# Grouped-query attention with an FFN on one NeuronCore: the value products of a group's last two pairs move to the next slot

## The reference

```python
# attention: 32 query heads, 8 key/value heads, head size 128
q = rope(layernorm(x) @ Wq);  k = rope(ctx @ Wk);  v = ctx @ Wv
attn = softmax(where(mask == 0, -1e9, q k^T / sqrt(128)))
x = x + concat_heads(attn @ v) @ Wo
# feed-forward: routed scales around a matrix of signs
h = layernorm(x)
routing = softmax(h @ gate_w.T)
out = (h * (routing @ in_scale)) @ sign(weight).T * (routing @ out_scale) + bias
x = x + out
```

## Time and profile before

| | |
|---|---|
| median of three executions | 1199.98 us (1199.96 to 1200.46) |
| the profiled execution | 1200.44 us, its span 1197.4 us |
| PE busy | 1162.7 us, 97% |
| VectorE busy | 810.1 us, 68% |
| GpSimd busy | 712.2 us, 59% |
| ScalarE busy | 551.7 us, 46% |
| mean granted TensorE clock | 0.988 |
| DMA, mean over the span | 89 GB/s |

### The profile page before, as it was taken

How to read it: one execution, slowest core, us unless ns; L and a number is a source line. 1 busy time by engine, 2 the same in 40 slices (tenths; PEclk the granted TensorE clock), 3 DMA queues, 4 the chain that set the end, 5 groups by cost and what they waited for, 6 DMA issues and landing times.

```text
span 1197.4 us, 23749 instructions
## 1 busy us (share of the span) xinstructions
PE 1162.7 (97%) x7636; PEld 951.1 (79%) x7636; DVE 810.1 (68%) x1367; ACT 551.7 (46%) x1768; POOL 712.2 (59%) x593
## 2 busy tenths in 40 slices
PE   5799999999999999999999999999999999999996
PEld 4588888888888888887888888888888888888875
DVE  6767677666776666676766677667667666666663
ACT  3445445444453544444544444544454354444432
POOL 5666655555666655765555675655666565676515
PEclk8899999999999999999999999999999999999997
DMA  8234332232422223433322322323332221222200
GB/s 219 86 110 119 96 98 87 80 92 80 120 89 71 79 79 88 128 101 93 98 76 72 95 90 77 105 80 96 88 98 88 62 79 62 87 83 89 66 2 35
DMA packets 136923, 106.02 MB, mean 89 GB/s; under 512 B 12776, under 2 KB 111080, under 8 KB 136864
## 3 DMA queue, kind: packets, MB, share of 16 engines
q1 hardware_dynamic: 131488, 94.78, 27.0%
q10 hardware_dynamic: 4608, 8.39, 2.1%
q0 software_dynamic: 768, 2.10, 0.5%
HBM read 101.05 MB, written 4.19 MB: 88 GB/s over the span
## 4 chain that ended last, share of the span: by engine, by line
PE 87%; DVE 9%; POOL 2%; issue 1%; ACT 1%; DMA 1%; POOLq 0%; DVEq 0%; SPq 0%; ACTq 0%
PE chunk L1037 23%; PE chunk L1038 22%; PE chunk L1039 22%; PE o_ps L1110 4%; DVE swp L793 3%; PE sc_ps L1085 3%; PE tr_ps L1085 2%; PE aux L1026 2%; PE o_ps L1026 2%; DVE qT L795 1%; PE sc_ps L1026 1%; PE tr_ps L1026 1%; PE aux L1187 1%; PE aux L1188 1%; DVE oT_lo L728 1%
## 5 line engine op out<-in xcount | busy, mean ns | idle before, releaser
L404 POOL TENSOR_TENSOR w_lo<-raw,w_hi 128x512 fp32r<-128x512 f32 x192 | 247.2, 1299 | 385.3 <-ACT w_hi L503 385.3
L793 DVE TENSOR_TENSOR swp<-chunk,sinT 64x512 f32<-64x512 f32 x320 | 220.4, 689 | 98.7 <-PE chunk L1039 94.7
L1037 PE MATMUL chunk<-xT_hi,w_hi 128*128 128x512 f32 (+1 forms) x512 | 211.6, 413 | 2.0 <-POOL w_lo L404 1.9
L1038 PE MATMUL chunk<-xT_lo,w_hi 128*128 128x512 f32 (+1 forms) x512 | 201.9, 394 | 0.0
L1039 PE MATMUL chunk<-xT_hi,w_lo 128*128 128x512 f32 (+1 forms) x512 | 201.1, 393 | 0.0
L1037 PE MATMUL chunk<-wo_hi,oT_hi 128*128 128x512 f32 x496 | 196.6, 396 | 0.4 <-issue 0.4
L411 POOL TENSOR_TENSOR qT<-qT,swp 128x512 f32<-128x512 f32 x128 | 165.9, 1296 | 47.1 <-DVE qT L795 44.9
L1039 PE MATMUL chunk<-wo_hi,oT_lo 128*128 128x512 f32 x496 | 193.7, 390 | 0.0
L1038 PE MATMUL chunk<-wo_lo,oT_hi 128*128 128x512 f32 x496 | 193.2, 390 | 0.0
L539 ACT ACTIVATE probs<-scores,neg_max 128x64 f32<-128x64 f32 x512 | 170.4, 335 | 28.2 <-DVE neg_max L750 28.2
L735 DVE TENSOR_TENSOR acc<-chunk,acc 128x512 f32 (+1 forms) x128 | 88.2, 689 | 139.9 <-PE chunk L1039 139.5
(11 more groups left out here) (281 smaller groups left out, 1936.7 us busy)
## 6 DMA issues: line engine op xcount, KB each, us to landing
raw<-in_L_xattn_Wo SPq DMA_DIRECT2D x132, 256.0 KB, 2.6
raw<-in_L_xattn_Wq SPq DMA_DIRECT2D x128, 256.0 KB, 2.7
raw<-in_L_xattn_Wk SPq DMA_DIRECT2D x32, 256.0 KB
raw<-in_L_xattn_Wv SPq DMA_DIRECT2D x32, 256.0 KB
acc<-in_x ACTq DMA_DIRECT2D x16, 256.0 KB, 2.9
c_tile<-in_ctx SPq DMA_DIRECT2D x12, 256.0 KB, 3.1
x_tile<-in_x SPq DMA_DIRECT2D x12, 256.0 KB, 3.4
result<-y ACTq DMA_DIRECT2D x12, 256.0 KB, 2.1
```

What stands on the lines that cost most here:

```text
L404: nc.gpsimd.tensor_tensor(lo, raw[:, n % RING, :], hi.bitcast(F32), ALU.subtract).then_inc(wsplit_lo, 1)
L793: last = nc.vector.tensor_tensor(swp[to, k, :], bank[of, :], sinT[to, here], ALU.mult)
L1037: nc.tensor.matmul(bank, a_hi, b_hi, start=i == 0, stop=False)
L1038: nc.tensor.matmul(bank, a_hi, b_lo, start=False, stop=False)
```

## The change

The block `values(s, 1)`, the value products of a group's pairs 2 and 3, leaves its place between `project(3)` and `project(4)` and runs in the next slot, between `out_proj(0)` and `v_rows`, through a small class `SlotBefore` that has the number of the slot before. What takes its output moves along: `out_hi` 2 and 3 on ScalarE to the place ahead of `v_in_rows`, `out_lo` 2 and 3 on VectorE to the place ahead of `v_lo_split`. Since the `o_ps` banks are in use then, V's transposes get a bank of their own, `chunk[2]`: `v_rows` waits for the last rotation out of that bank, and `out_proj(2)`, the next to write to it, waits for `v_ok`. `t_rows` and `values(s, 0)` get waits for the subtractions out of the `o_ps` banks. In FFN slots `scale_in` goes from behind `rotate(2)` to ahead of it. GpSimd's and SyncE's queues stay as they are. The diff shows `slot(s)` of ScalarE, VectorE and TensorE in this order; their `attend_last(s)` get the same added lines at the same places, on ScalarE behind its four `split_hi`.

```diff
-        DUO_BANK, V_BANK, TABLE_BANK = [sc_ps, tr_ps], o_ps[0], o_ps[1]
+        DUO_BANK, V_BANK, TABLE_BANK = [sc_ps, tr_ps], chunk[2], o_ps[1]
...
+        class SlotBefore:
+            def __init__(self, s):
+                self.U = s.U - 1
+                self.late = True
...
             def out_hi(s, p):
                 act.wait_ge(pv_done, (s.U - 1) * DUOS + p // 2 + 1)
-                if not s.first_attn:
+                if s.late:
+                    act.wait_ge(outproj_done, (s.U - 1) * PAIRS + 1)
+                elif not s.first_attn:
...
             def slot(s):
...
                     split_hi(s, 1)
+                if s.wo:
+                    out_hi(SlotBefore(s), 2)
+                    out_hi(SlotBefore(s), 3)
                 if s.attn:
                     v_in_rows(s)
...
                     xs_split(f[0], in_slot)
-                if s.attn:
-                    out_hi(s, 2)
-                    out_hi(s, 3)
-                if s.ffn:
                     out_scales(f[0], in_slot)
...
             def slot(s):
...
                     add_out(s, 0)
+                    out_lo(SlotBefore(s), 2)
+                    out_lo(SlotBefore(s), 3)
                 if s.attn:
                     v_lo_split(s)
...
                     out_lo(s, 1)
+                if s.ffn:
+                    scale_in(f[0], in_slot)
                 if s.proj:
                     rotate(s, 2)
-                if s.ffn:
-                    scale_in(f[0], in_slot)
...
                     rotate(s, 3)
-                if s.attn:
-                    out_lo(s, 2)
-                    out_lo(s, 3)
...
                 elif p == 1:
                     pe.wait_ge(vT_ok, s.U)
+                elif p == 2:
+                    pe.wait_ge(v_ok, s.U)
...
             def v_rows(s):
                 pe.wait_ge(vT_ok, s.U)
-                if not s.first_attn:
-                    pe.wait_ge(o_lo, (s.U - 1) * PAIRS)
+                pe.wait_ge(cos_done, s.U * KQ)
...
                 if d == 0:
                     pe.wait_ge(v_ok, s.U)
+                    if not s.first_attn:
+                        pe.wait_ge(o_lo, 2 * n)
...
-            def t_rows(t):
+            def t_rows(s, t):
                 pe.wait_ge(rows_in, 16 * (t - PAIRS + 1))
+                if s.wo:
+                    pe.wait_ge(o_lo, (s.U - 1) * PAIRS)
...
             def slot(s):
...
                     out_proj(s, 0)
+                    values(SlotBefore(s), 1)
                 if s.attn:
                     v_rows(s)
...
                     t_out_scales(f, in_slot)
-                if s.attn:
-                    values(s, 1)
                 if s.proj:
                     project(s, 4)
```

More of the change, by code:

```diff
@@ L219, in __init__ @@
                 self.ffn, self.intake, self.residual = ffn, intake, residual
+                self.late = False
                 side = q % 2
@@ L1231, in slot @@
                 if s.intake:
-                    t_rows(t)
+                    t_rows(s, t)
                     t_x(t)
```

## The result

The changed kernel takes 1217.28 us in the median of four executions (1216.14 to 1218.1) beside 1199.97 for the kernel before: a ratio of 1.0147, with 1.0135 to 1.0159 as its 95% interval. It is slower by 17.3 us where 17.1 was forecast. The profiled execution has a span of 1215.2 us against 1197.4, so the traces differ by 17.8, and TensorE's mean granted clock is 0.993 against 0.988: no time was lost to the clock.

The account below looks back on a forecast made before the run. PE, busy for 97%, was taken as the bound, with POOL's splits as the second. 18.8 - 1.7 + 0.4 = +17.5, less 0.4 hidden, gave +17.1: 1217.1 us, range 1208.5 to 1224.

Parts of the forecast that it names:

- The second bound: POOL's split_lo(9) ends at A + 6.57, A being the start of project(3)'s last matmul; out_proj(0) starts 0.27 us later.
- Taking the block out: Non-FFN slots, 19 times: removing the block is worth 0.06 us, not 1.16, as out_proj(0) waits for POOL's splits.
- Putting it back: Between out_proj(0) and v_rows, 31 times: the block costs 1.05 us, ends 0.97 to 1.10.
- FFN slots: Twelve FFN slots: 1.19 us saved despite a stall on xs_lo, 1.05 paid later; net -0.14 each, -1.7 in all.
- ScalarE and VectorE: Copies and subtractions delay the softmax chain about 2.4 us; covered in full slots, out_proj(2) keeping 0.7 us room on v_ok.
- The end: Slot after the last projection: chain moves 2.4 us, PE 1.05, with 1.0 of room at probs_T(0); stall of 0.4 us.
- The slot in which PE already came late: One slot, where PE came late by 0.5 us, can hide part of its stall: -0.4 us.
- (a): At out_proj(0) of the 19 slots: POOL isn't in the way, no stall; 1196.6 us (1191.8 with xs_lo in time); chance 0.07.
- (b): out_proj(2) also stalls on v_ok behind the 12 FFN slots: 6 us, 1223 us; chance 0.13.
- (c): Half the stall: the block costs the low end and xs_lo doesn't bind; +8.6, 1209 us; chance 0.08.

Follow-up runs that it names:

- the splits ahead: Changed kernel with GpSimd's split_lo(8) and split_lo(9) moved ahead of rope_sum(3): 1196.77 us, ratio 0.9974.
- the one with both orders and the block in its old place: Kernel before with scale_in ahead of rotate(2), split_lo 8 and 9 ahead of rope_sum(3), xs_lo_split ahead of rope_sum(2): 1193.49 us, ratio 0.9953.
- with both orders: Changed kernel with split_lo 8 and 9 ahead of rope_sum(3) and xs_lo_split ahead of rope_sum(2): 1193.08 us; 1192.51 on a second chip.
- the move alone: Changed kernel with scale_in back behind rotate(2) and split_lo 8 and 9 ahead of rope_sum(3): 1198.02 us, ratio 0.9979.

## Why the prediction was right

**The second bound.** The step that decides was to set POOL's end, A + 6.57, beside PE's arrival. After: A + 6.56, and 18 stalls on it. It was told by a small thing in the trace of before, a weight load 0.1 us later than the stream's; the split that was taken out of its way in the kernel before (the load is back at 0.23 us) and the added microsecond on POOL show that it meant what it was read as.

**Taking the block out: +0.06 forecast.** PE would have been ready at 538.54, that is A + 5.69 (5.68 forecast); released at A + 6.70 (6.70), second matmul A + 7.03 (7.01). That is 0.04 us per slot instead of 0.06.

**Putting it back: 1.05.** Measured 0.99 + 0.06 on the first transposes. Taking the middle between no loss and 0.11 there was a guess, and it came out; the low end of 0.97, and with it 0.84 and 1.15 for a slot, had no row behind them. The whole 1.16 of the old place isn't paid again: with the splits ahead the slots came out 0.09 and 0.14 us shorter than before. Entry and exit cost the same in both places (0.32 and 0.90 with the block between them); what is saved lies behind the exit, in the matmuls that follow. The nineteen slots together came to +19.0, beside 18.8 - 0.4.

**FFN slots: -0.14 each.** Measured -0.11, -1.4 us in all against -1.7. Ending the wait for `scale_in` did bring the wait for `xs_lo`; the release was 0.14, and `xs_lo` ended 3.39 us behind the start of the projection's last matmul, where it was 3.37 before. **ScalarE and VectorE.** `out_proj(2)` never waits for `v_ok`. VectorE's and PE's timelines in the slot behind an FFN slot:

```profile
400.42 0.68 DVE L739 TENSOR_TENSOR v_lo<-chunk,v_hi 128x512 fp32r<-128x512 f32 x1
...
401.94 0.39 PE L1049 MATMUL chunk<-wo_hi,oT_hi 128*128 128x512 f32 x1
```

`v_lo` ends at 401.10, with 0.84 us of room where 0.7 was worked out from the earlier trace rows; it is the least room in any of slots 2 to 31. **The end:** +0.3 us against +0.4. The stall itself is smaller: `probs_T(0)` starts 0.37 us behind the matmul ahead of it instead of 0.23.

**Mis-sized.** The slot in which PE already came late was to hide 0.4 us of its stall; it is 0.90 longer where the others with intake are 1.05, so it hid 0.15. The hiding as such was read rightly: in the kernel before with the added work on POOL, PE starts 0.15 us behind POOL's end in this slot as in the others, and it is 0.37 longer instead of 1.02. In the changed kernel PE's own lateness there grew, and that was nowhere in the prediction (last heading). With the FFN slots, which gave back 0.3 us less than forecast, this is most of what the sum of +17.1 lacks to the traces' +17.8.

**Luck.** That the medians differ by 17.3 us, 0.2 from the forecast, says less than it seems: the executions of the changed kernel alone spread over 2 us, and the first slot with attention, which counts in the sum, varies by more than 2. The mechanism is carried by the slots' lengths and not by this agreement.

**The rivals.** (a), without the stall, was put at 1196.6; the changed kernel with the splits ahead is that case, and takes 1196.77. So the rival's price was right and its condition false. (b) and (c) didn't occur: no wait on `v_ok`, and both the block and `xs_lo` cost what the likeliest case said.

## What to carry to other kernels

Before work is taken out of the engine that looks like the bound, look for the wait that comes next in its queue and for how long that has been met: here 0.27 us at 59% occupancy of the other engine turned a gain of 0.1 us per slot into a loss of 1.0. Two edits that each end a wait must be priced together, since each may hide the other's: moving `scale_in` was worth 5 us with the block in its place and no more than about 1 us with the block moved. When a move fails on such a wait, look at the order of the *other* engine's queue first; two lines moved there were worth 20 us.

## What was not expected of the hardware

At one slot, where the loop over the middle quarters goes from its first pass to its second, PE idles ahead of `out_proj(0)` for a reason that no semaphore explains. PE's timelines there: the kernel before, the one with both orders and the block in its old place, the changed kernel with the splits ahead, with both orders, and with the block behind the scores:

```profile
565.56 0.49 PE L1037 MATMUL chunk<-wo_hi,oT_hi 128*128 128x512 f32 x1 [0.36 <-issue]
```

```profile
564.49 0.49 PE L1038 MATMUL chunk<-wo_hi,oT_hi 128*128 128x512 f32 x1 [0.35 <-issue]
```

```profile
564.16 0.49 PE L1049 MATMUL chunk<-wo_hi,oT_hi 128*128 128x512 f32 x1 [1.61 <-issue]
```

```profile
562.62 0.49 PE L1050 MATMUL chunk<-wo_hi,oT_hi 128*128 128x512 f32 x1 [1.11 <-issue]
```

```profile
560.85 0.49 PE L1051 MATMUL chunk<-wo_hi,oT_hi 128*128 128x512 f32 x1 [1.33 <-issue]
```

It is 0.24 to 0.36 us in the kernels with the block in its old place and POOL not late, and 1.1 to 1.6 in every kernel in which the block was moved and POOL isn't late (1.52 in the move alone). In the changed kernel it is 1.33, the longest of the waits shown under the result, 0.61 us past POOL's end. It takes about 1 us from the gains of the kernels with the block moved, once. It isn't the jump of just any loop: the inner loops over the groups jump back at the same place in the slot, and in the changed kernel with the splits ahead `out_proj(0)` follows there at 0.22 to 0.23 us like anywhere else. That it is this longer jump, or the loading of the code behind it, is argued from the place alone; no run here varied it, and why the moved block makes it longer stays open. The first slot with attention also varies without a cause that I can name: from its `v_rows` to the next it was 30.2 to 33.3 us long in these traces, in no order that follows the edits. Spans of single executions can't be compared more finely than about 1 us.
